# A gated cross-attention and mixture-of-experts kernel: routing four batches in one chain

## The chip, the cores and the metric

The kernel runs on one core of a Trainium2 chip. The metric is the device time of one execution in microseconds. The engines are PE (TensorE), DVE (VectorE), ACT (ScalarE), POOL (GpSimd) and SP (SyncE, which here only issues transfers).

## The reference, cut

32 batches of 112 latent rows of 256 numbers attend to 375 context rows and to themselves (8 heads of 64), with a mask. Then each row goes to the best 2 of 8 experts.

```python
x = x + jnp.tanh(g_xattn[0]) * _L0_xattn_ref(ctx_1024, _layernorm(x), mask_BxS2_bk0, L0_xattn_kv_gate, ...)
x = x + jnp.tanh(g_ffn[0]) * _L0_ffn_ref(_layernorm(x), L0_ffn_conf_w, L0_ffn_conf_b, ...)

def _L0_ffn_ref(x, conf_w, conf_b, gate_w, up_w, down_w, wealth):
    bids = jax.nn.sigmoid(jnp.einsum('bsh,eh->bse', x, conf_w) + conf_b) * wealth
    top_bids, selected_experts = jax.lax.top_k(bids, 2)
    routing_weights = jax.nn.softmax(top_bids, axis=-1)
    combine = jnp.sum(jax.nn.one_hot(selected_experts, 8) * routing_weights[..., None], axis=2)
    expert_out = jax.vmap(ffn)(gate_w, up_w, down_w)   # down(silu(gate x) * (up x)), 1024 wide
    return jnp.einsum('ebsh,bse->bsh', expert_out, combine)
```

## The kernel before

All engines run their own instruction streams, tied by semaphores. Each stream is written in the order in which it runs, so the place of a line in the body is its place in the queue. Numbers of 32 bits go through PE as a high and a low half: ACT makes the high half out of PSUM (L650, L638), DVE the low half (piece_lo, L849), POOL the low half of the normalized rows (rows_lo, L457, zTs).

**Attention phase (to about 945 us).** It is a chain of bodies b = 0 to 33, each with eight head slots h = 0 to 7. Body b computes the scores, the row maxima (masked_max, L859), the exponentials, the transposed probabilities (probs_lo, L865) and the values of batch b; and beside them the output of batch b-1 (heads_out L877, residual L890 to L897, norm2 L903), the projections q, k, v of batch b+1 (piece, L1205; the first of them starts a body in the text below), the transposed rows of batch b+2 (rows_T) and the statistics of batch b+3 (norm_stats; rstd on POOL, L443 to L451; norm_rows on ACT in h5 and h6, L620). Bodies 0 and 1 and 28 to 33 are written out; bodies 2 to 27 are a loop over two bodies (13 iterations).

**Routing.** In each odd body from 3 on, the pair of batches (b-3, b-2) is routed on DVE, in tiles of 112 rows by 2 batches by 8 experts: choose (14 steps in h2 to h4, spread by CHOOSE_AT; L926 is step 0, L931 and L933 the next), route_rank in h5 (after ranks on PE, L1307 to L1311), route_weights in h6, route_place in h7. Nearly every step waits for the one before it on the same engine (after_last, link). Then POOL's scatter (L498) writes the pair's rows to the lists of the experts with four indirect transfers.

**POOL's order in a body** is: mask_bias, rows_lo, rstd, rstd1 (L471, L474), scatter in an odd body, then split_weights (L481, a copy, and L484, a subtraction, of 128x1536), which prepares a 32nd of the expert weights; SP stores it and loads the next piece.

**The end.** In body 31 (h5) DVE sorts the experts by their number of rows (order_experts) and gives SP the first free row of each list (pad_rows, L1011, L1012). SP waits for it, writes eight blocks of empty rows (L373) behind the lists and then loads the first expert's weights (load_expert(0), L366). The last pair (30, 31) is routed in body 33. The expert phase is 63 tiles of 128 rows.

Of the kernel before, what the change touches and what calls it, by code (L numbers as in the profile page):

```python
# [5 lines left out]
F32 = mybir.dt.float32  # L6
# [8 lines left out]
P = 128  # L15
# [40 lines left out]
assert AHEAD * P * E <= 2 * (TOK - 2 * S)  # L56
# [3 lines left out]
RCHAIN = 26  # L60

CHOOSE_AT = {2: (2, 2, 1), 3: (2, 2, 1), 4: (2, 1, 1)}


def build(nc, x, ctxt, mask, scal, lnw, wqkv, wout, confw, confbw, wffn, out):
# [4 lines left out]
    with ctx:  # L70
# [6 lines left out]
        def psum(name, shape, stack):  # L77
# [7 lines left out]
        counts = sb("counts", [S, E], F32)  # L85
# [7 lines left out]
        pad_row_f = sb("pad_row_f", [1, E], F32)  # L93
# [25 lines left out]
        regoff_b = sb("regoff_b", [S, E], F32)  # L119
        first_pref = sb("first_pref", [S, E], F32)  # L120
        tok_id = sb("tok_id", [S, 2], F32)
        zrow = sb("zrow", [S, 2, 2, XW], F32)
        lg = sb("lg", [S, 2, E], F32)
        ex = sb("ex", [S, 2, E], F32)
        bids = sb("bids", [S, 2, E], F32)
        tmp = sb("tmp", [S, 2, E], F32)
        top = sb("top", [S, 2, 2], F32)
        pick = sb("pick", [S, 2], F32)
        oh = sb("oh", [S, 2, 2, E], F32)
        both = sb("both", [S, 2, E], F32)  # L130
        gap = sb("gap", [S, 2], F32)
        gexp = sb("gexp", [S, 2], F32)
        w1 = sb("w1", [S, 2], F32)
        wt = sb("wt", [S, 2, 2], F32)
        slot = sb("slot", [S, 2, E], F32)
        slot_c = sb("slot_c", [S, 2, 2], F32)
        slot_i = sb("slot_i", [S, 2, 2], I32)
# [54 lines left out]
        z2 = [sb(f"z2_{i}", [S, D], F32, pa) for i in range(2)]  # L192
# [14 lines left out]
        rank_P = ptP[1][0:S, 0, S:P]  # L207
        tot_P = ptP[1][0:S, 1, S:S + E]
# [44 lines left out]
        s_rexp, s_route, s_oh, s_gexp, s_rank, s_slots, s_zcopy, s_scat = [sem(n) for n in (  # L253
            "s_rexp", "s_route", "s_oh", "s_gexp", "s_rank", "s_slots", "s_zcopy", "s_scat")]
# [37 lines left out]
        def _(sp):  # L292
# [91 lines left out]
            sp.wait_ge(s_scat, 64 * PAIRS)  # L384
# [15 lines left out]
        def _(pool):  # L400
# [13 lines left out]
            nc.gpsimd.memset(counts[:, :], 0.0)  # L414
# [71 lines left out]
            def scatter(pair):  # L486

                pool.wait_ge(s_slots, pair + 1)
                pool.wait_ge(s_zcopy, pair * 2 + 2)
                if isinstance(pair, int) and pair == PAIRS - 1:  # L490

                    pool.wait_ge(s_padw, 16 * E)
                    for t in range(AHEAD):
                        pool.wait_ge(s_xt[t], 16)
                apart(pool)
                for p in range(2):
                    for c in range(2):
                        pool.indirect_dma_start(xs[:, :], bass.IndirectOffsetOnAxis(ap=slot_i[:, c, p:p + 1], axis=0),  # L498
                                                zrow[:, p, c, :], None).then_inc(s_scat, 16)
# [12 lines left out]
            def body(b, p, j=None):  # L512
# [10 lines left out]
                if isinstance(b, int) and b == B:  # L523

                    pool.wait_ge(s_order, 1)
                    pool.wait_ge(s_padw, 16 * E)
                    pool.wait_ge(s_scat, 64 * (PAIRS - 1))
# [17 lines left out]
            body(0, 0)  # L545
            body(1, 1)
            with pool.Fori(1, PAIRS - 2) as j:
                body(j * 2, 0, j)
                body(j * 2 + 1, 1, j)
            for b in range(B - 4, B + 2):  # L550
                body(b, b % 2)
# [20 lines left out]
            pool.wait_ge(s_scat, 64 * PAIRS)  # L572
# [14 lines left out]
        def _(act):  # L587
# [893 lines left out]
```

## Time and profile before

| | us |
|---|---|
| median of 3 runs | 1609.39 (1608.31 to 1612.14) |
| profiled execution | 1617.49 |
| its span | 1615.8 |
| PE busy, share of the span | 1430.9, 89% |
| DVE busy | 953.8, 59% |
| ACT busy | 843.5, 52% |
| POOL busy | 601.9, 37% |
| mean granted PE clock | 0.971 |

The busy shares are means over two phases: DVE is busy some 80 to 90% of the attention phase and 20 to 30% of the expert phase, PE above 90% in most of both. A row of a timeline gives the start from the beginning of the span, the length, engine and line, what is written from what, the shapes, and in brackets the idle time of the engine ahead of it with what ended it. Matmuls that follow each other are merged into one row (xN).

### The profile page before, as it was taken

The page shows a single profiled execution, that of the slowest core. Times are in us where ns is not written, and L with a number is a line of the kernel's source. Part 1 is how long each engine was busy: PE and PEld are TensorE (multiplying, and loading weights), DVE is VectorE, ACT ScalarE, POOL GpSimd, SP SyncE. Part 2 cuts the span into 40 slices and gives each one's busy share as a digit, 9 for nine tenths or more (in the row PEclk, how much of TensorE's full clock was granted, in tenths as well). Part 3 has the DMA queues.
Part 4 walks back from the last instruction along what each step waited for, and adds up shares of the span by engine and source line. Part 5 has one row for each costly group of instructions (what it writes and reads, how often), then busy time and mean ns, then how long its engine had stood idle before and what let it go on. Part 6 is the DMA issues. An engine that isn't in the chain of part 4 may idle for free.

```text
span 1615.8 us, 39656 instructions
## 1 busy us (share of the span) xinstructions
PE 1430.9 (89%) x11944; PEld 1086.9 (67%) x11945; DVE 953.8 (59%) x2651; ACT 843.5 (52%) x1873; POOL 601.9 (37%) x666
## 2 busy tenths in 40 slices
PE   1999998999899989998998569999999999999946
PEld 1566665666566656665655457888888788888835
DVE  4688888888888888888886632333332223333211
ACT  4777786778677867776775312232332223323311
POOL 5344564455546553654354212222222222222211
PEclk9999999999999999999999779999999999999977
DMA  4132433243334333423343569211114751111182
GB/s 131 49 124 92 152 128 118 99 155 121 117 104 158 111 115 112 161 99 119 119 139 115 171 209 276 49 29 26 28 28 133 228 181 29 27 29 27 33 263 69
DMA packets 70908, 180.59 MB, mean 112 GB/s; under 512 B 11664, under 2 KB 33552, under 8 KB 70864
## 3 DMA queue, kind: packets, MB, share of 16 engines
q1 hardware_dynamic: 54464, 153.66, 28.3%
q0 software_dynamic: 15264, 24.25, 7.6%
q10 hardware_dynamic: 1136, 2.12, 0.4%
q8 instruction: 24, 0.39, 0.1%
q14 instruction: 20, 0.16, 0.0%
HBM read 106.91 MB, written 73.09 MB: 111 GB/s over the span
## 4 chain that ended last, share of the span: by engine, by line
PE 63%; DVE 13%; issue 9%; DMA 8%; ACT 2%; another core or an unknown queue 1%; POOL 1%; DVEq 1%; SPq 1%; ACTq 0%; POOLq 0%
PE fP L1205 14%; PE yP L1205 10%; PE gP L1205 10%; PE uP L1205 9%; DMA W<-split_experts 4%; PE simP L1253 4%; PE ptP L1263 3%; PE aP L1388 3%; PE oP L1205 3%; PE tP L1205 3%; DVE pT L865 2%; DMA out<-ysb,xt 2%; DVE ms L859 1%; DMA xt<-routed_rows 1%
## 5 line engine op out<-in xcount | busy, mean ns | idle before, releaser
L1144 DVE TENSOR_TENSOR act_h<-uP,sg 128x512 f32<-128x512 f32 x126 | 87.1, 691 | 295.2 <-ACT sg L757 295.2
L1205 PE MATMUL gP<-W,xT 128*128 (+1 forms) x756 | 212.5, 417 | 37.8 <-issue 30.0
L1205 PE MATMUL fP<-zTs,ws 128*128 128x112 f16 (+1 forms) x1536 | 220.8, 294 | 23.3 <-DVE kT L849 12.9
L757 ACT ACTIVATE sg<-gP 128x512 f32<-128x512 f32 x126 | 75.4, 598 | 296.0 <-PE uP L1205 294.2
L558 POOL DMA_INDIRECT out<-ysb,xt x63 | 100.6, 1597 | 280.0 <-ACT ysb L769 265.0
L859 DVE CUSTOM_DVE_ANT_0 ms<-simP,madd,sim_undo 112x488 f32<-112x488 f32 x256 | 184.5, 721 | 34.3 <-remote 19.0
L1205 PEld LDWEIGHTS yP<-W,aT 128*128 128x128 f32 x1512 | 192.5, 194 | 10.1 <-issue 5.3
L1205 PE MATMUL yP<-W,aT 128*128 (+1 forms) x1512 | 194.3, 286 | 4.6 <-DVE aT L1148 4.6
L1205 PE MATMUL uP<-W,xT 128*128 (+1 forms) x756 | 197.0, 397 | 0.0
L1205 PE MATMUL fP<-ws,zTs 128*128 128x512 f16 x768 | 186.9, 379 | 10.3 <-DVE kT L849 10.1
L657 ACT ACTIVATE pr<-ms,nmax 112x488 f32<-112x488 f32 x256 | 179.2, 700 | 30.1 <-DVE nmax L859 26.4
L1205 PEld LDWEIGHTS fP<-zTs,ws 128*128 128x128 f16 x1536 | 109.9, 99 | 116.0 <-issue 31.8
L1148 DVE TENSOR_TENSOR aT<-aP,aT 128x512 fp32r<-128x512 f32 x126 | 86.4, 686 | 164.9 <-ACT aT L763 164.9
L1205 PEld LDWEIGHTS gP<-W,xT 128*128 128x128 f32 x756 | 136.9, 194 | 64.4 <-issue 41.9
L664 ACT ACTIVATE pT<-ptP 122x448 f16<-122x448 f32 x256 | 138.1, 539 | 73.3 <-PE ptP L1263 69.3
L865 DVE SCALAR_TENSOR_TENSOR pT<-ptP,pT 122x448 f16<-122x448 f32 x256 | 157.9, 617 | 25.8 <-ACT pT L664 17.1
L1205 PEld LDWEIGHTS uP<-W,xT 128*128 128x128 f32 x756 | 145.5, 192 | 32.4
L763 ACT ACTIVATE aT<-aP 128x512 fp32r<-128x512 f32 x126 | 75.1, 596 | 172.4 <-PE aP L1388 172.4
L1205 PE MATMUL oP<-v,pT 122*128 122x64 f16 x3072 | 133.5, 194 | 20.9 <-DVE ao L877 19.7
L1263 PE MATMUL ptP<-ident,pr 112*122 112x112 f32 x1024 | 142.9, 262 | 0.0
L1205 PEld LDWEIGHTS oP<-v,pT 122*128 122x128 f16 x3072 | 123.7, 98 | 26.6 <-issue 16.2
L1263 PEld LDWEIGHTS ptP<-ident,pr 112*122 112x122 f32 x1024 | 115.5, 141 | 25.0 <-ACT pr L657 1.2
(204 smaller groups left out, 2261.4 us busy)
## 6 DMA issues: line engine op xcount, KB each, us to landing
split_experts<-wparts SPq DMA_DIRECT2D x32, 1536.0 KB, 6.6
W<-split_experts SPq DMA_DIRECT2D x64, 768.0 KB
wr<-wffn SPq DMA_DIRECT2D x32, 768.0 KB, 8.0
xc<-ctxt SPq DMA_DIRECT2D x32, 375.0 KB
xt<-routed_rows POOLq DMA_DIRECT2D x63, 129.0 KB, 2.4
xl<-x SPq DMA_DIRECT2D x32, 112.0 KB
xres<-x SPq DMA_DIRECT2D x32, 112.0 KB, 7.8
out<-x SPq DMA_DIRECT2D x32, 112.0 KB, 1.9
```

Of the source, the lines that this page charges most:

```text
L558: pool.indirect_dma_start(out[:, :], bass.IndirectOffsetOnAxis(ap=xt[k][:, D:D + 1].bitcast(I32), axis=0), ysb[k % 2][:, :], None, compute ...
L657: nc.scalar.activation(pr[h % 2][:, :], ms[h % 2][:, :], ACT.Exp, bias=nmax[p][:, h:h + 1], scale=-1.0, accum_out=rsum[p][:, h:h + 1]).the ...
L664: nc.scalar.activation(pT[h % 2][:, 0, :, 0:S], ptP[h % 2][0:KR, :, 0:S], ACT.Copy, scale=P_TOP).then_inc(s_pthi, 1)
L757: nc.scalar.activation(sg[i][:, :], gP[i][:, :], ACT.Silu).then_inc(s_silu, 1)
L763: nc.scalar.activation(aT[q][i][:, 0, :, :], aP[i][:, :, :], ACT.Copy).then_inc(s_athi, 1)
L859: nc.vector.tensor_tensor_reduce(out=ms[h % 2][:, :], in0=simP[h % 2][0:S, 0:NK], in1=madd[p][:, :], scale=sim_undo[0:S, 0:1], scalar=3.0e ...
L865: nc.vector.scalar_tensor_tensor(out=pT[h % 2][:, 1, :, 0:S], in0=ptP[h % 2][0:KR, :, 0:S], scalar=P_TOP, in1=pT[h % 2][:, 0, :, 0:S], op0 ...
L1144: nc.vector.tensor_tensor(act_h[i][:, :], uP[i][:, :], sg[i][:, :], ALU.mult).then_inc(s_act, 1)
L1148: nc.vector.tensor_tensor(aT[q][i][:, 1, :, :], aP[i][:, :, :], aT[q][i][:, 0, :, :].bitcast(F32), ALU.subtract).then_inc(s_atlo, 1)
L1205: last = nc.tensor.matmul(o, lhs(k, a), rhs(k, c), start=n == 0, stop=n == len(todo) - 1)
L1253: last = nc.tensor.matmul(simP[i][:, 0:NK], qT[p][r, a, h // 2, :], kT[p][r, c, h // 2, :], start=t == 0, stop=t == len(PARTS) - 1)
L1263: last = nc.tensor.transpose(ptP[h % 2][0:KR, c, 0:S], pr[h % 2][:, c * KR:(c + 1) * KR], ident[0:S, 0:S])
```

## The change

- Four batches (a quad) are routed in one chain, in tiles of 112 by 4 by 8. The tables zrow, oh, slot and the rest have four batches; z2 has four buffers.
- The loop has four bodies (b = 4 to 27, 6 iterations); bodies 0 to 3 and 28 to 33 are written out. With g = b mod 4, quad q-1 is routed in the bodies g = 1, 2 and 3 of quad q: QUAD_AT gives the steps at (g, h), each placed right behind the row maxima of that slot. g = 0 has none, and body 3 routes nothing.
- Steps are merged: the two rank-and-place halves work on both choices at once (at_slot, slot_c), the list's start is held in filled, the weights are written straight into zrow. A quad takes 28 DVE instructions; two pairs took 66. The rank takes eight matmuls for four batches; two pairs took ten.
- The scatter of a quad is eight indirect transfers in g = 3: four ahead of split_weights, four behind.
- The last four batches are routed as pairs, (28, 29) in bodies 31 and 32, (30, 31) in body 33.
- pad_rows moves from body 31, h5, to body 32, h3, behind route_rank of the pair (28, 29), and so counts that pair too. order_experts stays and works with the counts through batch 27.

```diff
-CHOOSE_AT = {2: (2, 2, 1), 3: (2, 2, 1), 4: (2, 1, 1)}
+QUAD_AT = {(1, 2): (0, 1), (1, 3): (2, 3), (1, 4): (4,), (1, 5): (5,), (1, 6): (6,), (1, 7): (7,),
+           (2, 0): (8,), (2, 1): (9,), (2, 2): (10,), (2, 3): (11,), (2, 4): (12, 13),
+           (3, 0): (16,), (3, 1): (17,), (3, 2): (18,), (3, 3): (19,), (3, 4): (20,)}
...
-                if p == 1 and holds(b, 3, B + 1):
-                    scatter((b - 3) // 2 if isinstance(b, int) else j - 1)
+                if quad:
+                    scatter(q - 1, 0)
                 if holds(b, 0, B - 3):
                     need(pool, s_z2, b)
                     split_weights(b)
+                if quad:
+                    scatter(q - 1, 1)
...
+                elif step == 8:
+
+                    link(nc.vector.scalar_tensor_tensor(out=bids[:, rows, :], in0=oh[:, 0, rows, :], scalar=-3.0e38, in1=bids[:, rows, :],
                                                         op0=ALU.mult, op1=ALU.add))
...
+            def weigh_choice(n, rows, step):
+
+                if step == 16:
+                    dve.wait_ge(s_gexp, n + 1)
+                    link(nc.vector.tensor_scalar(w1[:, rows], gexp[:, rows], 1.0, None, ALU.add))
+                else:
+                    after_last(n)
+                    link(nc.vector.reciprocal(w1[:, rows], w1[:, rows]))
+
+            def place(n, rows, step):
+
+                after_last(n)
+                width = rows.stop - rows.start
+                if step == 18:
+
+                    for half in range(2):
+                        if rows.start <= half * 2 < rows.stop:
+                            need(dve, s_scat[half], (QUADS - 1 if rows.stop - rows.start == 2 else n) * 64)
+                    nc.vector.tensor_scalar(zrow[:, rows, 0, D + 1:D + 2], w1[:, rows].unsqueeze(2), gates[0:S, 1:2], None, ALU.mult)
+                    nc.vector.scalar_tensor_tensor(out=zrow[:, rows, 1, D + 1:D + 2], in0=w1[:, rows].unsqueeze(2), scalar=gates[0:S, 1:2],
+                                                   in1=gexp[:, rows].unsqueeze(2), op0=ALU.mult, op1=ALU.mult)
+                    nc.vector.tensor_copy(zrow[:, rows, :, D:D + 1].bitcast(I32).rearrange("p g c w -> p g (c w)"),
+                                          tok_id[:, rows].unsqueeze(2).to_broadcast([S, width, 2]))
+                    link(nc.vector.tensor_tensor(at_slot[:, :, rows, :], oh[:, :, rows, :],
+                                                 slot[:, rows, :].unsqueeze(1).to_broadcast([S, 2, width, E]), ALU.mult))
...
+            def ranks(n, lo, hi, busy):
+
+
+                pe.wait_ge(s_oh, n + 1)
+                pe.wait_ge(s_ptlo, busy)
+                nc.tensor.matmul(rank_P[:, lo:hi, :], earlier[:, :], both[:, lo:hi, :], start=True, stop=False)
+                for g in range(1, hi - lo):
+                    nc.tensor.matmul(rank_P[:, lo + g:hi, :], ones[0:S, 0:S], both[:, lo:hi - g, :], start=False, stop=g == hi - lo - 1)
+                for g in range(lo, hi):
+                    last = nc.tensor.matmul(tot_P, ones[0:S, 0:S], both[:, g, :], start=g == lo, stop=g == hi - 1)
+                last.then_inc(s_rank, 1)
...
-            with pe.Fori(1, PAIRS - 2) as j:
-                body(j * 2, 0)
-                body(j * 2 + 1, 1, j - 1)
+            for b in range(4):
+                body(b, b, 0)
+            with pe.Fori(1, QUADS - 1) as q:
+                for g in range(4):
+                    body(q * 4 + g, g, q)
```

What it does to the order of instructions is shown at three places. In these rows ms and nmax are the row maxima, qT, kT and v the low halves of the projections, pT those of the probabilities, bids and oh the experts' bids and the chosen ones; REGISTER_ALU and ISA rows are the waits' bookkeeping.

DVE, start of a body (h0) without routing, before:

```order
L859 ISA ms,nmax<-simP,madd,sim_undo 112x488
L859 ISA nmax 112x1
L840 ISA
L849 SCALAR_TENSOR_TENSOR qT<-fP,qT 128x2x112
L840 REGISTER_ALU
L849 SCALAR_TENSOR_TENSOR qT<-fP,qT 128x2x112
```

The same place in the body g = 2, after:

```order
L899 ISA ms,nmax<-simP,madd,sim_undo 112x488
L899 ISA nmax 112x1
L276 REGISTER_ALU
L986 SCALAR_TENSOR_TENSOR bids<-oh,bids 112x32
L880 ISA
L889 SCALAR_TENSOR_TENSOR qT<-fP,qT 128x2x112
L880 REGISTER_ALU
L889 SCALAR_TENSOR_TENSOR qT<-fP,qT 128x2x112
```

Step 8 now stands between the first row maxima and the low halves of qT.

DVE, h2 of an odd body of the loop, before:

```order
L854 REGISTER_ALU
L859 ISA ms,nmax<-simP,madd,sim_undo 112x488
L859 ISA nmax 112x1
L870 RECIPROCAL rinv<-rsum 112x8
L926 TENSOR_SCALAR tmp<-ex 112x16
L269 ISA
L931 RECIPROCAL bids<-tmp 112x16
L840 REGISTER_ALU
L849 SCALAR_TENSOR_TENSOR kT<-fP,kT 128x488
L840 REGISTER_ALU
L849 SCALAR_TENSOR_TENSOR kT<-fP,kT 128x488
```

DVE, h2 of the body g = 3, after:

```order
L899 ISA ms,nmax<-simP,madd,sim_undo 112x488
L899 ISA nmax 112x1
L910 RECIPROCAL rinv<-rsum 112x8
L276 REGISTER_ALU x2
L1028 TENSOR_SCALAR zrow<-w,gates 112x4
L1029 SCALAR_TENSOR_TENSOR zrow<-w,gates,gexp 112x4
L1031 CAST zrow<-tok_id 112x8
L1033 TENSOR_TENSOR at_slot<-oh,slot 112x64
L880 REGISTER_ALU
L889 SCALAR_TENSOR_TENSOR kT<-fP,kT 128x488
L880 REGISTER_ALU
```

Two instructions of routing stood ahead of the low halves of kT, each with one input; now the four of step 18 stand there.

DVE, in body 31, before:

```order
L1004 TENSOR_REDUCE region<-placed 1x8
L1006 TENSOR_SCALAR first_f<-turn,region 1x4
L1007 CAST first_i<-first_f 1x4
L1011 TENSOR_TENSOR pad_row_f<-counts,reg_off 1x8
L1012 CAST pad_row_i<-pad_row_f 1x8
L890 SCALAR_TENSOR_TENSOR x_0<-tP,gates,xres 112x256
L893 BN_STATS bn<-x_0 112x6
L897 BN_AGGR mv<-bn 112x2
```

DVE, in body 32, after:

```order
L905 SCALAR_TENSOR_TENSOR pT<-ptP,pT 122x4x112
L910 RECIPROCAL rinv<-rsum 112x8
L917 TENSOR_TENSOR ao<-oP,rinv 112x512
L1006 TENSOR_TENSOR slot<-ptP,filled 112x16
L1008 TENSOR_TENSOR filled<-filled,ptP 112x8
L1071 CAST pad_row_i<-filled 1x8
L1014 TENSOR_SCALAR w<-gexp 112x2
L1017 RECIPROCAL w<-w 112x2
L922 SCALAR_TENSOR_TENSOR aoT<-tP,aoT 128x448
```

The cast of the pad rows has moved from behind order_experts to behind the rank of the pair (28, 29).

## Rows read from the trace of the kernel before

**Rows 1.** Stretches start:end: length, busy time (instructions) per engine, clock, DMA share, GB/s.

```profile
100.15:124.72 24.57, 24.27 (x256) 16.07 (x254) 21.14 (x55) 19.78 (x47) 12.22 (x15) 1.00 0.38 129
124.72:153.19 28.47, 25.34 (x266) 17.18 (x264) 24.91 (x79) 20.81 (x51) 10.82 (x13) 1.00 0.34 113
424.42:450.39 25.97, 24.49 (x257) 16.21 (x255) 21.39 (x64) 19.46 (x45) 17.66 (x20) 1.00 0.40 138
450.39:478.65 28.26, 25.34 (x266) 17.18 (x265) 24.88 (x79) 20.80 (x51) 10.85 (x13) 1.00 0.33 111
```

**Rows 2.** Waits of PE, 260 to 803 us: releaser, total us, times, longest.

```profile
PE fP L1205 <- DVE kT L849: 16.0, 20, 0.9
```

**Rows 3.** Timeline of DVE: start, length, instruction [idle before it <- releaser].

```profile
107.06 0.67 DVE L849 SCALAR_TENSOR_TENSOR kT<-fP,kT 128x488 f16<-128x488 f32 x1 [0.63 <-ACT kT L650]
...
114.32 0.66 DVE L849 SCALAR_TENSOR_TENSOR kT<-fP,kT 128x488 f16<-128x488 f32 x1
...
466.14 0.18 DVE L943 TENSOR_TENSOR tmp<-tmp,first_pref 112x16 f32<-112x16 f32 x1
```

**Rows 4.** Timeline of PE, bodies 2 and 15 (matmuls, merged).

```profile
115.12 1.46 PE L1205 MATMUL fP<-ws,zTs 128*128 128x512 f16 x6
...
469.65 0.27 PE L1307 MATMUL ptP<-both,earlier 112*112 112x8 f32 x2
...
470.37 0.34 PE L1311 MATMUL ptP<-both,ones 112*112 112x8 f32 x2
```

**Rows 5.** Timeline of POOL, bodies 2, 3 and 31.

```profile
106.74 2.47 POOL L457 TENSOR_TENSOR zTs<-zT,zTs 128x1200 f16<-128x1200 f32 x1 [1.95 <-ACT zTs L638]
...
124.70 3.48 POOL L484 TENSOR_TENSOR wparts<-wr,wparts 128x1536 fp32r<-128x1536 f32 x1 [0.18 <-POOL wparts L481]
...
892.95 1.47 POOL L481 CAST wparts<-wr 128x1536 fp32r<-128x1536 f32 x1 [7.05 <-DMA wr<-wffn]
894.59 3.42 POOL L484 TENSOR_TENSOR wparts<-wr,wparts 128x1536 fp32r<-128x1536 f32 x1 [0.18 <-POOL wparts L481]
```

**Rows 6.** Timeline of DVE, bodies 3 and 31.

```profile
125.47 0.72 DVE L859 CUSTOM_DVE_ANT_0 ms<-simP,madd,sim_undo 112x488 f32<-112x488 f32 x1
...
893.98 0.46 DVE L926 TENSOR_SCALAR tmp<-ex 112x16 f32<-112x16 f32 x1
...
894.76 3.28 DVE L933 TENSOR_TENSOR bids<-bids,confb 112x16 f32<-112x16 f32 x1
```

**Rows 7.** Timeline of POOL, body 14.

```profile
444.25 0.24 POOL L451 TENSOR_SCALAR shift<-shift 128x4 f32<-128x4 f32 x1 [0.20 <-POOL shift L450]
```

**Rows 8.** Timeline of ACT, body 2.

```profile
119.55 1.08 ACT L620 ACTIVATE z<-xc,shift,rs 125x256 f32<-125x256 f32 x2
```

**Rows 9.** Stretches: bodies 28 to 31 together, then 30 and 31.

```profile
804.21:917.28 113.07, 92.06 (x960) 63.32 (x959) 86.56 (x263) 66.89 (x158) 46.98 (x39) 0.93 0.35 125
857.77:890.52 32.75, 26.08 (x264) 17.01 (x263) 19.97 (x55) 16.55 (x40) 15.72 (x11) 0.95 0.43 149
890.52:917.28 26.76, 16.21 (x184) 12.88 (x181) 21.80 (x75) 11.51 (x31) 5.69 (x4) 0.75 0.34 129
```

**Rows 10.** Timeline of PE, body 30.

```profile
886.40 0.41 PE L1292 MATMUL tP<-ident,z 112*128 112x112 f32 x2 [4.75 <-DVE z L903]
```

**Rows 11.** Timeline of POOL, body 30.

```profile
864.52 1.48 POOL L481 CAST wparts<-wr 128x1536 fp32r<-128x1536 f32 x1
```

**Rows 12.** Timeline of SP's queue, body 31.

```profile
913.04 9.71 SPq L373 DMA_DIRECT2D routed_rows<-padrows  x8
```

**Rows 13.** Timeline of PE, first matmuls of the expert phase.

```profile
946.58 2.90 PE L1205 MATMUL gP<-W,xT 128*128 128x512 f32 x6 [7.79 <-DMA W<-split_experts]
```

**Rows 14.** Page, part 6, DMA issues: count, KB each, median us to landing.

```profile
wr<-wffn SPq DMA_DIRECT2D x32, 768.0 KB, 8.0
...
xt<-routed_rows POOLq DMA_DIRECT2D x63, 129.0 KB, 2.4
```

**Rows 15.** Page, part 3, DMA queues: packets, MB, share of 16 engines.

```profile
q8 instruction: 24, 0.39, 0.1%
```

More of the change, by code:

```diff
@@ L510, in load_tile, with body @@
                 pool.dma_start(xt[k][:, :], xs[bass.ds(row, P), :]).then_inc(s_xt[k], 16)
-            def body(b, p, j=None):
+            def body(b, g, q):
+                p = g % 2
+                quad = g == 3 and holds(b, 7, B - 1)
                 if isinstance(b, int) and B - 2 <= b < B:
@@ new lines, in choose @@
+                c, m = (0, step - 3) if step < 8 else (1, step - 9)
+                if step == 1:
+                    link(nc.vector.reciprocal(bids[:, rows, :], tmp[:, rows, :]))
+                elif step == 2:
+                    link(nc.vector.tensor_tensor(bids[:, rows, :], bids[:, rows, :], per_expert(confb[:, 1, :], rows), ALU.mult))
+                elif step == 8:
+                    link(nc.vector.scalar_tensor_tensor(out=bids[:, rows, :], in0=oh[:, 0, rows, :], scalar=-3.0e38, in1=bids[:, rows, :],
@@ new lines, in choose, with route_rank @@
+                if step == 13:
+                    after_last(n)
+                    nc.vector.tensor_tensor(gap[:, rows], top[:, 1, rows], top[:, 0, rows], ALU.subtract)
+                    nc.vector.tensor_tensor(both[:, rows, :], oh[:, 0, rows, :], oh[:, 1, rows, :], ALU.add).then_inc(s_oh, 1)
+            def route_rank(n, rows):
+                dve.wait_ge(s_rank, n + 1)
+                link(nc.vector.tensor_tensor(slot[:, rows, :], rank_P[:, rows, :], per_expert(filled[:, :], rows), ALU.add))
+                after_last(n)
+                link(nc.vector.tensor_tensor(filled[:, :], filled[:, :], tot_P, ALU.add))
@@ L1019, in tlink, with body @@
                 dve.wait_ge(s_tabch, tchain[0])
-            def body(b, p, j=None):
+            def body(b, g, q):
+                p = g % 2
+                routing = holds(b, 5, B - 1)
                 for h in range(H):
-                    routing = p == 1 and holds(b, 3, B + 1)
-                    if routing:
-                        pair_ = (b - 3) // 2 if isinstance(b, int) else j - 1
-                    def choose_some(point):
-                        if routing and h in CHOOSE_AT:
-                            done = sum(sum(CHOOSE_AT[i]) for i in CHOOSE_AT if i < h) + sum(CHOOSE_AT[h][:point])
-                            for n in range(done, done + CHOOSE_AT[h][point]):
-                                choose(pair_, n)
                     if h == 3 and holds(b, 1, B):
```

355 lines of the change are left out of this document (180 added, 175 removed).

## The prediction

> **What bounds the kernel now.** I read the stretches between starts of a body's first projection on TensorE (PE) first [rows 1]. Until 917 us PE has 24.27 us of work in the 24.57 us of a body without routing: PE is the bound there, and anything that lengthens a body beyond 24.57 us is a wait of PE or work added to it. A routed odd body takes 28.26 to 28.47 us. An even body of the loop does no routing, yet takes 25.97: it carries the scatter of the pair before it. So a pair of batches costs 25.97 + 28.26 = 54.23 us, four batches 108.5, and two unrouted bodies would be 49.1: routing costs 5.1 us a pair, 51 us or so in the ten pairs of the middle.
>
> PE's waits from 260 to 803 us say where this arises [rows 2]: 16.0 us, the largest sum, for the low halves of kT, which VectorE (DVE) makes. DVE is not full (24.9 of 28.3 us busy in a routed body), but it works in order, and each link of the routing chain sits ahead of something that PE wants. In h2 to h4 the low half of kT has no slack: it ends at 114.98 and PE's next projection starts at 115.12 [rows 3, 4]. So an instruction put before it costs its full time, less DVE's own idle time in that slot. A chained link of 112x16 takes about 0.2 us (0.18 at 466.14) for 16 elements a row, where the low half of kT moves 488 in 0.66: that is overhead and not data, so 112x32 costs little more. In the rank step PE itself has work: five tiny matmuls, the first at 469.65 and the last at 470.37, 0.18 to 0.20 apart [rows 4].
>
> **The change, part by part.** The sum is made on the profiled run, 1617.49 us (span 1615.8), which is 8.1 us or 0.5% above the median of the runs shown, 1609.39; the difference is taken over to that median.
>
> (1) Body 3 no longer routes: 28.47 becomes 24.57 [rows 1]. **-3.9 us.**
>
> (2) The four bodies of the new loop. Each quad takes 28 DVE instructions where two pairs took 66, now spread over bodies g=1 to g=3.
> g=1 (steps 0 to 7, one a slot, two in h2 and h3). DVE idles 0.24 to 0.8 us in most of these slots of an unrouted body, which covers one link; the second link in h3 (0.3) and the one in h4 (0.1) are not covered. 24.57 + 0.43 = **25.0 us**.
> g=2. Steps 9 to 11 are mostly covered: 0.15. In h4 stand steps 12 and 13, gap and both, 0.67. The rank is eight matmuls for five at 0.20 each, 1.6 us on PE [rows 4]. Then step 8: it is a SCALAR_TENSOR_TENSOR with two inputs in SBUF, straight after the first row maxima and before the low halves of qT, for which PE waits. In the stretch after a body starts, GpSimd (POOL) runs the second half of split_weights, L484, from 0.02 before to 3.46 after that start (124.70 to 128.18 for a body that starts at 124.72) [rows 5]. DVE's masked maxima, with one input in PSUM, run beside it undisturbed (125.47, 0.72 us), but L933, two inputs in SBUF, took 3.28 us at 894.76 and ended with L484 [rows 5, 6]. Step 8 would be reached at 1.40 after the start and be let go at 3.46: 2.06, less DVE's small reserve, 1.88. Together 24.57 + 0.15 + 0.67 + 1.6 + 1.88 = **28.9 us**; without the collision 27.0.
> The Trainium skill states this as a rule (SBUF — State Buffer, "Practical consequences"): an instruction of VectorE with two SBUF inputs contends with one of GpSimd that reads SBUF. The 3.28 us agree. It speaks against where the change puts these two steps; a SCALAR_TENSOR_TENSOR of this kind is in no row, so that the rule covers it is the page's word.
> g=3. Step 18 stands after L870's counterpart in h2 (it ends at 106.43, 0.63 before the row at 107.06, in a body that starts at 100.15; so 6.3 after the start), and its last instruction, a TENSOR_TENSOR of 112x64, has two SBUF inputs. POOL's zTs runs from 6.59 to 9.06 after the start [rows 3, 5]. The low halves of kT queue behind it: the collision begins near 6.8 and holds them 2.3 us, of which the 0.63 idle before 107.06 covers some: 1.67. Steps 19 and 20 cost 0.05: 24.57 + 1.67 + 0.05 = **26.3 us**; without the collision 24.7.
> g=0 has no routing, but POOL now scatters eight rows' worth of lists for four: four ahead of split_weights, which need no longer wait for a slot at the body's end, and four behind it. Before, POOL's chain that gives the next rows' scale ended at 444.49, 20.1 after the start of the body at 424.42 [rows 7]; with one scatter starting some 5 us earlier and the other added behind the splits it ends some 21 after, and ACT's norm_rows (19.4 after the start in an unrouted body, 119.55 [rows 8]) waits 1.55 us for it. That is as much as the 1.4 us that a scatter costs an even body now, and a little more for ACT: 26.3, between 25.6 and 27.5. Sum of a quad in steady state: 26.3 + 25.0 + 28.9 + 26.3 = 106.5 against 108.5: -2.0, five times (the quads routed in bodies 9 to 27, with one more scatter): **-10.0 us**. The first one (bodies 4 to 7) has no scatter in front, 24.6 for g=0: 104.8 against 108.5: **-3.7 us**.
>
> (3) Bodies 28 to 31. They took 113.07 us together [rows 9]. Body 30 (32.75) holds a 4.75 us wait of PE for z before 886.40 [rows 10], which comes from POOL: its split stands behind a scatter and starts at 864.52 only [rows 11], and the next split waits for a load of weights that starts only when this one is done. Body 29 now routes no pair, so that scatter is gone from there, and the splits come about 4.8 us earlier: 28.0. Body 31 keeps its chain but loses part of the 3.1 us that L933 lost to L484: 24.8. With 26.3 and 25.0 for 28 and 29: 104.1: **-9.0 us** (from -3, if body 30 keeps its wait, to -12).
>
> (4) pad_rows. It stood in body 31, ahead of body 32's start at 917.28 [rows 9]; SP issued the eight pad transfers from 913.04 on, 9.71 us, then the first expert's weights, for which PE's first expert matmul (946.58) waits 7.79 us [rows 12, 13]. Now pad_rows stands behind route_rank of the pair (28, 29) in h3 of body 32, behind the matmuls of its rank: some 5.8 + 1.1 after that body's start. SP's pads start about 7.2 after it instead of 4.24 before: **+11.4 us** straight on the path, as SP does nothing else and the weights are issued behind the pads (9 to 13).
>
> (5) The loop closes 5 times over four bodies for 12 times over two. PE's loop holds twice the instructions, some 2,200 by the order of the programs. The trace has nothing on an edge of such a loop: DVE shows 0.63 us of issue time at an edge, and PE none that can be seen. From both sides: 0, and 2.4 us, in which the smallest transfers of a similar kind (129 KB) land [rows 14]. A refill of one 16 KB piece (24 packets, 0.39 MB in the whole run [rows 15], no packet of that queue between 260 and 800 us) is smaller than that, so I take the middle, 1.2: **+6 us** (0 to +12).
> The Trainium skill (Runtime: NRT & Kernel Launch, instruction memory) gives PE room for 2048 instructions, refilled in blocks of 16 KiB in sequence. The packets of [rows 15] have that size. By the page the old loop fits and the new one does not, and each edge would cost a fetch.
>
> Sum: -3.9 - 3.7 - 10.0 - 9.0 + 11.4 + 6 = -9.2: 1608.3 for the profiled run, **1600.2** for the median.
>
> **Rivals.** (A) Step 16, a TENSOR_SCALAR of 112x4 with one input, in h0 of g=3, stands under L484 in the same place as step 8. For it: L926, a TENSOR_SCALAR of 112x16, took 0.46 us at 893.98 where 0.12 is usual, and ended with the CAST of POOL that started at 892.95 and lasted 1.47 [rows 5, 6]. Against: 112x2 ones take 0.16, longer than the 0.12 of 112x16, so the small ones seem to run in another mode. Price: 1.8 x 6 = +10.8: 1611.
> (B) Slower. If PE has to fetch not one piece but a row of them at a loop's edge, while its transfers share the queues with the weights, an edge costs what a weight load takes to land, 6 to 8 us (wr lands in 8.0 [rows 14]) instead of 1.2: +5.1 x 5 = +25.5: 1625.7. It decides from 3.0 us an edge, where the time is equal to before, and shows as slower from 4.0. Against it: 16 KB are a fiftieth of that load.
> (C) Faster. Steps 8 and 18 do not collide, because the type or the time differs by the microsecond that it takes: -(1.88 + 1.67) x 6 = -21.3: 1579. Against it: 894.76.
>
> **Chances.** A difference of 0.3%, 4.8 us, is about what a measurement of this kernel can tell. Forecast (1592 to 1608) 0.38: of it 0.27 faster, 0.10 the same, 0.01 slower. A 0.22: 0.03, 0.13, 0.06. B 0.20: 0, 0.01, 0.19. C 0.20: all faster. Together 0.50 faster, 0.24 the same, 0.26 slower. The range has to take in A, half of C and half of B: 1580 to 1625.
>
> **What would show it.** Step 8 (the SCALAR_TENSOR_TENSOR on bids of 112x32) near 2 us, and the 112x64 TENSOR_TENSOR near 2.2, in all six quads; else (C). The TENSOR_SCALAR of 112x4 near 2 us: (A). A wait of PE at the start of every fourth body with instruction packets in the middle of the run: (5), and its length decides on (B). Body lengths of 26.3, 25.0, 28.9, 26.3. SP's pads 7.2 us after body 32 starts, and the first expert matmul as much later. The sum fails above all if the weights were not what the first expert matmul waits for, or if the waits of POOL in g=0 pass ACT's slack by more than the 1.5 us taken.

## The result

The changed kernel takes 1636.77 us (median of 4, 1632.79 to 1637.63) against 1610.77 for the kernel before on the same chip: a ratio of 1.0158, 95% interval 1.0138 to 1.0177. It is 26 us slower, outside the predicted range (1580 to 1625), and on the side of rival (B). A second measurement of the same program, told below, gave 1.009 (1.0053 to 1.0126): part of the loss changes from run to run.

The span of the profiled run is 1634.5 us. These are the stretches of the kernel after that answer to [rows 1] and [rows 9], as rows of windows (length, busy time by engine, granted PE clock, DMA share, GB/s): bodies 4 to 27 together, then bodies 15 to 19 (g = 3, 0, 1, 2, 3), then 27 and 28.

```profile
149.49:823.20 673.71, 614.38 (x6194) 410.98 (x6193) 551.78 (x1459) 478.37 (x1093) 333.61 (x377) 0.97 0.36 121
...
455.87:485.43 29.56, 24.58 (x257) 16.30 (x255) 24.52 (x65) 20.77 (x49) 15.54 (x18) 0.99 0.37 124
485.43:516.86 31.43, 28.58 (x257) 19.52 (x255) 20.67 (x53) 19.05 (x43) 16.67 (x20) 0.84 0.36 117
516.86:541.67 24.81, 24.31 (x256) 16.22 (x255) 22.45 (x63) 19.95 (x48) 12.30 (x15) 1.00 0.37 128
541.67:570.07 28.40, 26.08 (x273) 17.85 (x271) 24.06 (x65) 20.03 (x47) 12.28 (x15) 1.00 0.33 112
570.07:600.17 30.10, 25.05 (x256) 16.36 (x255) 24.53 (x65) 20.77 (x49) 16.06 (x18) 0.96 0.37 123
...
796.86:823.20 26.34, 24.45 (x256) 16.33 (x255) 23.79 (x64) 19.93 (x47) 12.79 (x15) 1.00 0.37 125
823.20:851.24 28.04, 24.84 (x256) 16.46 (x255) 21.38 (x55) 19.45 (x46) 19.62 (x22) 1.00 0.38 124
```

The same stretch of the kernel before took 651.02:

```profile
153.19:804.21 651.02, 598.03 (x6219) 400.73 (x6217) 555.43 (x1693) 483.29 (x1106) 342.38 (x384) 1.00 0.36 124
```

The bodies g = 1 and g = 2 are as forecast (24.8 for 25.0, 28.4 for 28.9). Body 27 has g = 3 and no edge behind it: 26.34, forecast 26.3. But a g = 3 body that ends in the loop's jump takes 29.6 to 30.4, and the g = 0 body behind it 27.6 to 31.9, with a granted clock of 0.83 to 0.96 in it. Up to the first expert matmul the two traces differ by body 3 -3.8 (24.65 for 28.47), bodies 4 to 27 +22.7, from there to the first expert matmul +7.3 (149.71 for 142.37): +26.3 with 0.1 ahead of body 3. The spans of the two profiled executions differ by 18.7 only (1634.5 and 1615.8), as the expert phase, which the change doesn't touch, took 661.6 in one and 669.2 in the other; the other kernels told here have 659 to 668 there. That the 26.3 equals the difference of the medians is chance to that extent.

PE at one of the five edges (body 15 to 16; start, length, instruction, idle time before it):

```profile
480.84 0.52 PE L1259 MATMUL oP<-v,pT 122*128 122x64 f16 x12
484.58 0.92 PE L1307 MATMUL simP<-kT,qT 64*128 64x488 f16 x6 [3.22 <-issue]
485.43 1.77 PE L1259 MATMUL fP<-zTs,ws 128*128 128x112 f16 x17
488.27 0.84 PE L1259 MATMUL fP<-zTs,ws 128*128 128x112 f16 x7 [1.07 <-issue]
488.89 0.96 PE L1317 MATMUL ptP<-ident,pr 112*122 112x112 f32 x4
```

In the text of the kernel the scores (L1307) are the first matmuls of a body, ahead of the first projection at which its start is read here. PE waits 3.22 us ahead of them for nothing that the trace knows ("issue"), 17 matmuls later once more for 1.07, in the middle of one product, where no semaphore stands. Then everything runs at about half speed: 0.96 us for four transposes that take 0.55 elsewhere, with a mean granted clock of 0.53, near the lower of its two levels (1.2 of 2.4 GHz):

```profile
484.50:494.00 9.50, 8.35 (x72) 7.42 (x73) 2.95 (x8) 1.94 (x5) 8.25 (x7) 0.53 0.38 139
```

What PE waited for is in the queues of instruction packets (q8, 16 KB each, and q14, 8 KB each). The whole run of the kernel after has, against [rows 15]:

```profile
q8 instruction: 87, 1.43, 0.4%
q14 instruction: 76, 0.62, 0.1%
```

and between 260 and 800 us, where before there was no such packet:

```profile
q8 instruction: 51, 0.84, 0.6%
q14 instruction: 44, 0.36, 0.2%
```

The kernel before had no packet of instructions in its loop; the kernel after has them in every pass. In PE's first wait of this edge (481.4 to 484.5 us) lies one packet of q8, and its share of the 16 engines' 3.1 us comes to 1.0 us:

```profile
q8 instruction: 1, 0.02, 2.1%
```

At the other four edges the first wait holds one such packet too, of 1.1 to 1.3 us. The packet is about as long as the prediction had priced it; the wait around it is three times as long.

### The profile page after: what moved, and what is told of

Read it like the earlier page. It is cut to its first block, busy times and chain, and to the rows that moved or that the text cites. A ratio compares the mean times of both kernels' runs of the same rounds, so it can differ in the third digit from the quotient of the medians.

```text
span 1634.5 us, 38750 instructions
## 1 busy us (share of the span) xinstructions
PE 1443.3 (88%) x11912; PEld 1093.2 (67%) x11913; DVE 947.0 (58%) x2367; ACT 838.2 (51%) x1859; POOL 599.4 (37%) x665
## 4 chain that ended last, share of the span: by engine, by line
PE 66%; DVE 9%; DMA 8%; issue 8%; ACT 5%; another core or an unknown queue 1%; SPq 1%; ACTq 0%; DVEq 0%; POOLq 0%; POOL 0%
PE fP L1259 16%; PE yP L1259 10%; PE gP L1259 9%; PE uP L1259 9%; PE simP L1307 4%; DMA W<-split_experts 4%; PE ptP L1317 4%; PE oP L1259 3%; PE aP L1448 3%; PE tP L1259 3%; DMA out<-ysb,xt 2%; ACT pr L683 2%; DMA xt<-routed_rows 2%; PE fP L1275 1%; DVE kT L889 1%
## 5 line engine op out<-in xcount | busy, mean ns | idle before, releaser
L1259 PE MATMUL fP<-zTs,ws 128*128 128x112 f16 (+1 forms) x1536 | 229.3, 302 | 22.8 <-POOL zTs L464 9.0
L1259 PEld LDWEIGHTS fP<-zTs,ws 128*128 128x128 f16 x1536 | 114.3, 102 | 120.9 <-issue 42.9
L1259 PEld LDWEIGHTS uP<-W,xT 128*128 128x128 f32 x756 | 144.7, 191 | 31.9
```

The lines of the kernel that those rows point to most:

```text
L1259: last = nc.tensor.matmul(o, lhs(k, a), rhs(k, c), start=n == 0, stop=n == len(todo) - 1)
```

## Experiments

The last column is read from the one profiled execution of each kernel.

| kernel | ratio to before | 95% interval | bodies 4 to 27, us |
|---|---|---|---|
| changed | 1.0158 | 1.0138 to 1.0177 | 673.7 |
| changed, measured again | 1.0090 | 1.0053 to 1.0126 | 666.0 |
| before, loop of four bodies (b_loop4) | 1.0228 | 1.0202 to 1.0254 | 688.8 |
| before, written out (b_flat) | 0.9989 | 0.9976 to 1.0003 | 640.8 |
| changed, written out (a_flat) | 0.9971 | 0.9955 to 0.9987 | 641.2 |
| changed, only PE written out (a_peflat) | 0.9982 | 0.9969 to 0.9995 | 642.5 |
| changed, two steps moved (a_moves) | 1.0022 | 1.0004 to 1.0041 | 653.8 |
| changed, weights ahead of pads (a_wfirst) | 1.0112 | 1.0072 to 1.0151 | 669.9 |
| changed, pads in body 31 (a_pads31) | 1.0050 | 1.0024 to 1.0077 | 653.0 |
| written out, pads in body 31 (a_flat_pads) | 0.9891 | 0.9851 to 0.9932 | 627.1 |
| written out, scatter behind (a_flat_behind) | 0.9933 | 0.9913 to 0.9953 | 633.7 |
| written out, moved, pads (a_best) | 0.9771 | 0.9750 to 0.9791 | 612.3 |
| the same, scatter behind (a_best2) | 0.9828 | 0.9812 to 0.9845 | 618.6 |

**The loop alone.** The kernel before, its routing untouched:

```diff
-            body(0, 0)
-            body(1, 1)
-            with pe.Fori(1, PAIRS - 2) as j:
-                body(j * 2, 0)
-                body(j * 2 + 1, 1, j - 1)
+            for b in range(4):
+                body(b, b % 2)
+            with pe.Fori(1, B // 4 - 1) as q:
+                for g in range(4):
+                    body(q * 4 + g, g % 2, q * 2 + (g // 2 - 1))
```

(and so for DVE, ACT and POOL).

> The kernel before, routing in pairs as it was, but with bodies 0 to 3 written out and a loop over four bodies. Theory F (fetch): the changed kernel lost its time at the edge of its loop, where PE's instructions are no longer held and must be fetched: about 5.9 us at each of 5 edges (a wait of 3.2 to 3.6 us, a second of 0.4 to 1.2, then a stretch at half clock). This kernel then takes 25 to 30 us more than before, 1636 to 1641, with instruction packets through the whole loop. Theory R (routing): the time went to the new routing, its eight transfers in a row on GpSimd and its colliding steps; this kernel then takes the time of before, 1611 within 5.

Measured: 1651.63 against 1613.57, +38 us. Its trace has the same picture, here at 495 us:

```profile
495.06 1.41 PE L1253 MATMUL simP<-kT,qT 64*128 64x488 f16 x6 [3.58 <-issue]
496.39 0.83 PE L1205 MATMUL fP<-zTs,ws 128*128 128x112 f16 x7
498.31 0.91 PE L1205 MATMUL fP<-zTs,ws 128*128 128x112 f16 x8 [1.08 <-issue]
...
496.39:526.86 30.47, 28.88 (x257) 19.79 (x255) 20.83 (x53) 19.29 (x43) 16.68 (x20) 0.82 0.35 120
```

Theory F holds and R falls: the larger loop costs this with no change in the routing. DVE waits for nothing that the trace knows as well, 3.3 to 3.8 us at each of these edges.

**No loop.** The 34 bodies of the changed kernel written out:

```diff
-            for b in range(4):
-                body(b, b, 0)
-            with pe.Fori(1, QUADS - 1) as q:
-                for g in range(4):
-                    body(q * 4 + g, g, q)
-            for b in range(B - 4, B + 2):
+            for b in range(B + 2):
                 body(b, b % 4, b // 4)
```

> The changed kernel with all 34 bodies written out and no loop in the attention phase. Theory F: no edge, no wait: 28 to 30 us less than the changed kernel, about 1607, if instructions that follow each other are fetched in time. Theory R: as the changed kernel, 1637.

Measured: 0.9971 for 1.0158: 1.9%, 30 us less. There is nearly as much instruction traffic as in the loop over four (74 packets of q8 for 87), and no wait of 3 us on PE in the bodies: here the stream in one direction is fetched in time, and the jump back wasn't.

**Only PE written out.** 

> The changed kernel with the bodies written out for PE alone; DVE, ACT and POOL keep the loop over four bodies. Theory F-PE: the cost of an edge is PE's fetch: the ratio to before falls to that of the kernel written out for all engines (0.997, about 1608). Rival: the other queue of instruction packets shows that another engine fetches in each turn as well; its wait at the edge then takes the place of PE's: 1618 or more, with a wait of DVE or ACT of 2 us or more once in four bodies.

Measured: 0.9982, as with all engines. PE's wait for its own instructions is gone. But what the rival expected shows as well: DVE, still in the loop, waits 2.6 to 2.9 us at each of the five edges with no cause but packets of q14 around it, and PE then waits 2.1 to 2.3 us for DVE's qT (body 16):

```profile
472.39 0.73 DVE L899 CUSTOM_DVE_ANT_0 ms<-simP,madd,sim_undo 112x488 f32<-112x488 f32 x1 [2.79 <-issue]
473.57 0.51 PE L1275 MATMUL fP<-ident,z 125*128 125x125 f32 x3 [2.24 <-DVE qT L889]
```

The g = 0 bodies behind an edge take 27.0 to 28.7. In the kernel written out for all engines DVE has no such wait, but these bodies take 27.9 to 28.9 for another reason (below), so the agreement of the two ratios says less than it seems. Against 25.5, which the body takes with neither, DVE's jump is worth 1.4 to 3.2 us an edge, an estimate from these lengths. So the jump costs most on PE, but not on PE alone.

**Before, written out** (the same edit).

> The kernel before with all 34 bodies written out: instructions of all engines come from memory through the whole phase, but there is no edge. Theory F: only a jump to a place that is not held costs; the stream itself is hidden, so this kernel takes the time of before within 5 us, and what the kernel with the new routing written out gains over it is the routing's own part (0.3%). Rival: fetches in a row cost something as well, as the waits of ACT and PE without a cause in the trace let suppose: 8 us or more above before, and the new routing is worth so much more.

Measured: 0.9989; theory F holds for the whole. But its pairs take 53.37 us instead of 54.23:

```profile
445.62:473.78 28.16, 25.34 (x266) 17.24 (x265) 24.85 (x79) 20.89 (x50) 10.60 (x13) 1.00 0.33 113
473.78:498.99 25.21, 24.37 (x256) 16.18 (x255) 21.43 (x64) 19.46 (x44) 17.84 (x20) 1.00 0.45 145
```

Bodies 4 to 27 take 640.76 for 651.02, 10.3 us or 0.86 a pair less. It is tempting to call this the edge of the small loop, as DVE shows 0.63 us of issue time there. But in b_loop4 an even body with no jump in front (g = 2, here body 14) is as long, without that wait of DVE, and so is the written-out body 28 of the kernel before (26.03):

```profile
439.06:465.00 25.94, 24.66 (x256) 16.15 (x255) 21.44 (x64) 19.47 (x45) 17.67 (x20) 1.00 0.43 140
```

So the 0.8 us of an even body are not the jump's; their cause is open. The medians move by 2 us only. Where the rest is given back I did not find; the profiled execution of the kernel before stands 8 us above the median of its runs.

**The two collisions.** Steps 8 and 16, one slot later:

```diff
-           (2, 0): (8,), (2, 1): (9,), (2, 2): (10,), (2, 3): (11,), (2, 4): (12, 13),
-           (3, 0): (16,), (3, 1): (17,), (3, 2): (18,), (3, 3): (19,), (3, 4): (20,)}
+           (2, 1): (8, 9), (2, 2): (10,), (2, 3): (11,), (2, 4): (12, 13),
+           (3, 1): (16, 17), (3, 2): (18,), (3, 3): (19,), (3, 4): (20,)}
```

> The changed kernel with step 8 moved from the first slot to the second of its body (beside step 9) and step 16 from the first slot to the second (beside step 17), out of the stretch in which GpSimd subtracts. Theory P (port): the two took 1.9 and 2.2 us instead of 0.2 in six quads; 1.8 to 2.0 us less for each on PE's path, 1637 - 22 = 1615. Rival: the body is bound by PE's other waits behind it and only part comes back, 1630 or more.

Measured: 1.0022 for 1.0158, 22 us less. In the changed kernel, DVE and POOL at the start of bodies 18 (g = 2) and 19 (g = 3) stand so (L986 is step 8, L1014 step 16, L1033 the last of step 18, L491 POOL's subtraction, L464 its zTs):

```profile
543.21 1.93 DVE L986 SCALAR_TENSOR_TENSOR bids<-oh,bids 112x32 f32<-112x32 f32 x1
545.06 0.68 DVE L889 SCALAR_TENSOR_TENSOR qT<-fP,qT 128x224 f16<-128x224 f32 x2
...
541.65 3.44 POOL L491 TENSOR_TENSOR wparts<-wr,wparts 128x1536 fp32r<-128x1536 f32 x1 [0.18 <-POOL wparts L488]
...
571.30 2.21 DVE L1014 TENSOR_SCALAR w<-gexp 112x4 f32<-112x4 f32 x1
573.42 0.67 DVE L889 SCALAR_TENSOR_TENSOR qT<-fP,qT 128x224 f16<-128x224 f32 x2
...
570.03 3.45 POOL L491 TENSOR_TENSOR wparts<-wr,wparts 128x1536 fp32r<-128x1536 f32 x1 [0.18 <-POOL wparts L488]
...
578.13 0.21 DVE L1033 TENSOR_TENSOR at_slot<-oh,slot 112x64 f32<-112x64 f32 x1
...
578.27 2.46 POOL L464 TENSOR_TENSOR zTs<-zT,zTs 128x1200 f16<-128x1200 f32 x1 [3.50 <-ACT zTs L664]
```

Both steps end with POOL's subtraction (545.09, 573.48), and the low halves of qT come behind them. Moved, they take 0.3 to 0.5 us. The bodies shrink from 28.4 to 27.15 (g = 2) and from 26.34 to 25.11 (g = 3, without an edge): 1.24 and 1.23 us, less than the 1.9 and 2.2 on DVE; where the difference goes was not traced. That is 15 us in all. The other 7 are not the moves': the edges' price came out smaller in this run (below), and against the second measurement of the changed kernel (1.0090) the gain is 11 us. Where there is no edge, the two kernels written out with the pads in body 31 (0.9891 and, moved, 0.9771) show it clean: bodies 4 to 27 go from 627.1 to 612.3, 14.8 us. Theory P holds, at two thirds of its size.

**Weights ahead of the pads.** In SP's queue, load_expert(0) ahead of the eight writes:

```diff
-            sp.wait_ge(s_padr, 1)
-            for e in range(E):
-                ...
             sp.wait_ge(s_plo, seq(B - 2, NPIECE))
             load_expert(0)
+            sp.wait_ge(s_padr, 1)
+            for e in range(E):
+                ...
```

(The other waits of load_expert, not shown, move with it.)

> The changed kernel with SP loading the first expert's weights ahead of the eight writes of empty rows instead of behind them. Theory W: the wait for the rank of the pair (28, 29) holds back the weights only because they stand behind it in SP's queue; the first expert matmul then waits for the routed rows instead (they landed about 10 us before the weights): 8 to 11 us less, 1627. Rival: the writes and the weights share the transfer engines and the rows come later by what the weights gain: 1634 or more.

Measured: 1.0112, its interval overlaps that of the changed kernel. The weights are issued 30 us earlier, at 920.28, but the first matmul is at 969.13 for 972.91, and at the start of body 28 it was 4.5 us ahead anyway:

```profile
920.28 22.76 SPq L373 DMA_DIRECT2D W<-split_experts  x8
943.82 11.64 SPq L385 DMA_DIRECT2D routed_rows<-padrows  x8
...
967.42 0.69 PE L1428 MATMUL xP<-ident,xt 128*128 128x128 f32 x2 [17.05 <-DMA xt<-routed_rows]
```

The wait turned into one for the routed rows, which can be read only when the pads are written. Theory W falls.

**Pads in body 31.**

```diff
-PADT = -(-(2 * S + P - 1) // P)
-CAP = TOK + PADT * P - 2 * S
+PADT = -(-(4 * S + P - 1) // P)
+CAP = TOK + PADT * P - 4 * S
...
                     if h == 5 and isinstance(b, int) and b == B - 1:
                         order_experts()
+                        pad_rows()
```

(with the wait for the pads ahead of scatter_pair, and without pad_rows in body 32).

> The changed kernel with the pad rows back in body 31, behind order_experts: they start at the counts through batch 27, each block has five tiles instead of three (so that it still reaches past the list's end), and the scatter of the pair (28, 29) waits for them. Theory W2: SP's pads and, behind them, the first expert's weights start some 17 us earlier; the first expert matmul comes about 10.5 us earlier in relation to the start of the last bodies, 1626 or 1.009 of before. Rival: eight blocks of 645 KB ahead of the weights take what the earlier start gives: within 4 us of the changed kernel.

Measured: 1.005, more gain than either expected, and at another place: bodies 4 to 27, which the edit doesn't touch, take 653.0 instead of 673.7, and the way from body 28 to the first expert matmul (946.79 - 802.49) 144.3 instead of 149.7.

**Placement or chance.**

> The changed kernel as it is, once more, with a second trace. The kernel with the pads in body 31 was 17 us faster instead of 10, and its trace shows 20.7 us less in bodies 4 to 27, which its edits do not touch, and 5.4 us less behind them. Theory L (placement): what an edge costs depends on where program and data lie in memory; the same kernel gives 1.016 again and 672 to 676 us for bodies 4 to 27. Rival (chance): it depends on the moment, and this trace can as well show 655 us; then the medians of single kernels with an edge carry 1% of chance.

Measured: 1616.54 (1611.38 to 1633.99) against 1603.75; its trace has 666.0 us for bodies 4 to 27. One and the same program is spread over 22 us, where the kernel before stays within 12: that speaks for chance, and against my theory L as I put it. But the first four executions lie within 5 us of each other, 22 to 27 us above the median of the kernel before on their chip, where six of these eight lie 8 to 19 us above theirs; so something that lasts through a measurement may have a part too; a variant that changed the size of the lists alone, to tell the two apart, gave no result. What differs at an edge can be read. Here is the edge of body 15 to 16, in the repeated run and then in the kernel with the pads in body 31, and behind each the clock around it:

```profile
479.64 0.80 PE L1307 MATMUL simP<-kT,qT 64*128 64x488 f16 x6 [3.46 <-issue]
483.09 0.84 PE L1259 MATMUL fP<-zTs,ws 128*128 128x112 f16 x7 [0.98 <-issue]
479.00:490.00 11.00, 9.38 (x80) 7.81 (x80) 4.88 (x13) 4.66 (x11) 9.67 (x8) 0.57 0.45 149
```

```profile
477.36 1.34 PE L1307 MATMUL simP<-kT,qT 64*128 64x488 f16 x6 [3.26 <-issue]
480.77 0.55 PE L1259 MATMUL fP<-zTs,ws 128*128 128x112 f16 x7 [0.38 <-issue]
476.00:490.00 14.00, 12.04 (x120) 8.21 (x121) 8.01 (x21) 8.04 (x18) 12.28 (x10) 0.88 0.51 151
478.63:504.55 25.92, 25.24 (x257) 16.81 (x255) 20.50 (x53) 18.96 (x43) 16.25 (x20) 0.96 0.43 141
```

The first wait is 3.3 to 3.5 us in both. Where the second is 0.98, PE then works at half clock for some 9 us; where it is 0.38, the clock is back at full by then. The second wait doesn't decide this, though: at the edge to body 12 of the kernel with the pads in body 31 there is none, and PE is at half clock for 8 us all the same:

```profile
365.73 1.40 PE L1307 MATMUL simP<-kT,qT 64*128 64x488 f16 x6 [3.69 <-issue]
367.07 2.42 PE L1259 MATMUL fP<-zTs,ws 128*128 128x112 f16 x24
367.00:376.00 9.00, 9.00 (x79) 7.90 (x78) 5.04 (x14) 5.10 (x11) 7.86 (x6) 0.55 0.50 166
```

The two bodies around the edge of body 15 to 16 take 59.7 us in the one and 55.95 in the other, against 52.0 undisturbed (26.35 and 25.65 in the repeated run): 7.7 and 4.0 us for an edge. Over the five edges it is 5.4 to 7.8 in the repeated run and 3.9 to 6.8 with the pads in body 31. In the first run it is 6.0 to 10.1; most of its g = 0 bodies there hold further waits of PE of 0.5 to 1.5 us, 8 to 12 us after their start. These are not in the repeated run, and body 28 of the first run, with no edge in front, is disturbed too (28.04 for 25.65). So a part of the first run's loss is the disturbance told below under g = 0 and not the jump. What decides the second wait and the clock stays open.

**Pads without an edge.**

> The kernel written out for all engines with the pads in body 31, which measures the pads without an edge. Against the kernel written out (0.9971): 10.5 us less by the forecast's term (0.9906), 5 us less by the trace of the looped one (0.994).

Measured: 0.9891 for the 0.9971 of the kernel written out, 13 us. In the trace the bodies 4 to 27 are 14.1 us shorter and the way from body 28 to the first expert matmul is 147.4 for 154.7. The first is not the pads' doing: it is the g = 0 body, 25.5 for 27.9 to 28.9. Nor is the second clearly: the kernels with only PE written out and with the scatter behind, pads in body 32, need 146.5 and 145.3 there. In this one the first matmuls wait for the routed rows, not the weights. So the pads' move back is worth between nothing and 7 us; the runs don't settle it.

**The body g = 0.** In the kernel written out, ACT waits in it, and PE in the midst of one product:

```profile
364.37 0.60 ACT L671 ACTIVATE qT<-fP 128x224 f16<-128x224 f32 x2 [2.37 <-remote]
...
363.58 0.19 PE L1244 MATMUL oP<-v,pT 122*128 122x64 f16 x1 [0.44 <-issue]
364.29 0.31 PE L1244 MATMUL oP<-v,pT 122*128 122x64 f16 x5 [0.52 <-issue]
```

```diff
-                if quad:
-                    scatter(q - 1, 0)
                 if holds(b, 0, B - 3):
                     need(pool, s_z2, b)
                     split_weights(b)
                 if quad:
+                    scatter(q - 1, 0)
                     scatter(q - 1, 1)
```

> The kernel written out for all engines, with all eight transfers of a quad behind split_weights instead of four ahead and four behind. In the body g = 0 PE takes 27.9 to 28.9 us where 26.3 were forecast, and ACT waits 2.3 us at 2.4 us after its start, when the first four transfers end. Theory S: the transfers ahead of split_weights do this, and body g = 0 falls by 1.5 us or more, 5 quads: 8 us less than the kernel written out. Rival: it is the length of POOL's work behind, and the body stays as it is or gets longer: no gain.

Measured: 0.9933 for 0.9971, 6 us; body g = 0 takes 26.53 and these waits are gone. But they are gone in the kernel written out with the pads in body 31 too, with the scatter as it was, at 25.55. So the edit doesn't cure the cause; it costs 1 us a quad and was without a disturbance of 2 to 3 in this run. Waits without a semaphore on two engines, while both have packets of instructions under way and the scatter's transfers run (362 to 363 us has one packet of q8 among 27 of q0), look like late fetches; that is argued, not shown.

**The parts together.** 

> The changed kernel with three edits together: written out for all engines, steps 8 and 16 moved by one slot, pads in body 31. If the three terms are independent, they add: 30 + 22 + 10 us below the changed kernel, about 1574, 0.977 of before. If the pads' earlier start or the moves gain nothing where PE no longer waits, 1585 or more.

Measured: 1567.19 against 1603.48, 0.9771: faster than both kernels. The sum came out as expected, though by parts of other sizes. Its quad, g = 0 to 3:

```profile
454.40:479.95 25.55, 24.36 (x257) 16.17 (x255) 21.17 (x55) 20.07 (x46) 19.60 (x22) 1.00 0.48 156
479.95:504.78 24.83, 24.32 (x257) 16.30 (x255) 22.55 (x63) 20.07 (x47) 12.28 (x15) 1.00 0.37 128
504.78:531.66 26.88, 25.96 (x272) 17.84 (x270) 22.46 (x65) 20.11 (x46) 12.27 (x15) 1.00 0.34 118
531.66:556.52 24.86, 24.34 (x256) 16.22 (x254) 22.10 (x64) 20.05 (x47) 12.81 (x15) 1.00 0.38 132
```

102.1 us for four batches, against 106.7 for two pairs of the kernel before written out: this is what merged routing with its two steps moved is worth, 4.6 us in four bodies.

> The best kernel so far (written out, steps 8 and 16 moved, pads in body 31) with the eight transfers of a quad behind split_weights. If the gain of that edit on the kernel written out (0.4% between the ratios) is its own, 0.973 of before, 1561; if it came from the two steps' collisions, whose place shifts against POOL's subtraction, nothing is left of it: 0.977.

Measured: 0.9828, worse than without the edit. Body g = 0 takes 26.57 for 25.55, and PE waits 1.74 us for z in it instead of 0.71: POOL's eight transfers now stand ahead of the scale that z needs. Both expectations were wrong, as the gain of 0.4% on the kernel written out was the absence of a disturbance.

## Why the prediction was wrong

**The step that failed is (5), the loop's edge.** It was named, and it was priced at 1.2 us, the middle of 0 and the landing of a small transfer. Measured, the first wait alone is 3.2 to 3.8 us, longer than the landing of 129 KB (2.4, [rows 14]) which I had taken as an upper end, though the one packet in it takes 1.0 to 1.3; a second wait of 0.3 to 1.4 follows at most edges; PE's clock is low behind them; and DVE has a wait of its own. The last three I didn't count at all. The two bodies around an edge are 3.9 to 10.1 us longer than the 52.0 undisturbed (after: 60.99 for bodies 15 and 16). Undisturbed, bodies 4 to 27 would take 104.1 + 5 x 105.2 = 630 us (25.65, 24.82, 28.4, 26.35, and 24.57 for body 4). They took 673.7: 8.7 us for each of five edges if all of it were theirs, but 2.0 us of the sum lie in body 10, at no edge, and more is in the disturbance of g = 0. It is 7.2 in the repeated run and 4.6 with the pads in body 31.
Rival (B), at a chance of 0.20, had the right side and about the right price (6 to 8 us, 1625.7), but not its mechanism: it let a row of pieces land as slowly as a weight load, and the trace has one packet of about 1 us in the first wait. That its price came close is luck. Its own time lay outside the range that was given.
The Trainium skill (Runtime: NRT & Kernel Launch, "Instruction fetch mechanics") gives PE room for 2048 instructions, refilled by sequential blocks of 16 KiB. The runs agree in that the loop over two bodies has no packet, the loop over four has 0.84 MB of them in 540 us in pieces of 16 KB, and a stream without a jump shows no such wait. The page calls the cost of a block's border mostly hidden and says that a jump to a place no longer held stalls for its fetch, without a price for it: the stream and the jump of these runs show both.

**(1), body 3:** -3.8 for -3.9.

**(2), the quads:** right in sum and in most parts, and a little too dear. Undisturbed 105.2 us instead of 106.5. g = 1: 24.8 for 25.0. g = 2: 28.4 for 28.9; step 8 took 1.93 us as forecast, but is worth 1.24 on PE's path, not 1.88. g = 3: 26.35 for 26.3, which is luck: step 18 did not collide, as zTs began 8.2 us after the body's start instead of 6.6; step 16 did, for 2.2 us, in all six quads. So rival (A) was right about its own step, and its price was cancelled by my error on the other. The doubt whether a small TENSOR_SCALAR is in another mode should have weighed less than the row of 0.46 us. Rival (C) falls for step 8 and holds for step 18. g = 0: 25.65 for 26.3 undisturbed.

**The even body of the kernel before.** I put the 1.4 us by which it exceeds an unrouted one down to the scatter. Written out it takes 25.21 instead of 25.97 with the same scatter, so 0.8 of the 1.4 is something else; it is not the jump, as shown above, and what it is stays open.

**(3) and (4):** the forecast was -9.0 + 11.4 = +2.4 from body 28 to the first expert matmul; it was +7.3, and 4.6 in the repeated run (962.27 - 815.28 = 147.0). Split at body 32, which starts at 929.08, (3) gave -7.2 (105.9 for 113.07) and (4) +14.5; in the repeated run -8.2 and +12.8, with the pads 7.2 us after that start (927.33 - 920.13), to the digit as forecast. In the first run SP's pads start 11.1 us after it, at 940.21, and the matmul waits for the weights as said:

```profile
940.21 9.38 SPq L380 DMA_DIRECT2D routed_rows<-padrows  x8
...
972.91 2.90 PE L1259 MATMUL gP<-W,xT 128*128 128x512 f32 x6 [9.70 <-DMA W<-split_experts]
```

But the claim that nothing else holds the matmul back was too strong: with the weights first, or the pads early, the rows take their place within a few us. In body 32 PE, ACT and, but for one step of 0.17 us, DVE stand still from 931 to 935 us with no cause in the trace, which the repeated run doesn't have; 4 us of the error are there.

## What to carry to other kernels

Before a loop body is made longer, count the instructions of each engine in it, the busiest first: here the loop over four bodies, which fetched its instructions anew in each pass, cost 4 to 10 us a pass, more than the merged work saved; written out, the same code was as fast as before, and with two steps and the pads moved 2.3% faster. Where a wait of some us falls on PE, look for what a lower clock costs behind it. And place small two-input or TENSOR_SCALAR steps of VectorE by what GpSimd does at that moment, since here they then cost not 0.2 us but the rest of its instruction (1.9 and 2.2 us).

## What the runs showed that I had not expected

- The wait at the jump (3.2 to 3.8 us, with one packet of 16 KB in it) is longer than the landing of a 129 KB load (2.4 us).
- PE's clock behind the jump was 0.53 to 0.57 for some 9 us at some edges and back at full within 3 us at others; the second wait, 17 matmuls later, does not tell which.
- With PE written out, DVE's own wait at the jump (2.6 to 2.9 us) stands on PE's path in its place.
- A TENSOR_SCALAR of 112x4 with a single input in SBUF takes 2.21 us beside a subtraction of GpSimd and ends with it, like one with two inputs.
- The looped kernel is spread over 22 us between the executions of one measurement; written out, over 9 (1605.3 to 1613.8).
